# The last state's accumulation moved off VectorE, new steps, and rows of the second block split in the tail, in a Mamba and gated MLP layer on one NeuronCore

## The reference, cut

```python
x_and_res = x @ W_in.T                      # x is layernormed
xp, res = jnp.split(x_and_res, 2, axis=-1)
xc = silu(causal_conv(xp, conv_w) + conv_b) # 4 taps, each channel alone
ssm = xc @ W_x.T                            # B (16), C (16), dt (1)
dt = softplus(dt @ W_dt.T + b_dt)
h = exp(A * dt_t) * h + dt_t * B_t * xt     # for each channel and state
y_t = einsum('bed,bd->be', h, C_t) + D * xt
x = x + silu(y + res) @ W_out.T
h = silu(lin(x, w1) * s1) * (lin(x, w2) * s2)   # x is layernormed again
h = gelu(lin(h, h1) * t1)
h = gelu(lin(h, h2) * t2)
x = x + lin(h, w3) * s3
```

## Time and profile before

| | us |
|---|---|
| runs, median of 3 | 2768.11 (2767.78 to 2770.92) |
| the profiled execution | 2766.63 |
| its span, first to last instruction | 2764.8 |
| TensorE busy | 2587.6 (94%) |
| VectorE busy | 2249.4 (81%) |
| ScalarE busy | 1970.6 (71%) |
| GpSimd busy | 1770.2 (64%) |

### The profile page before, as it was taken

The page is one execution under the profiler, slowest core; times in us unless marked ns, Lnnn a source line. Parts: engine busy times, 40 slices in busy tenths (PEclk is TensorE's granted clock), DMA queues, the critical chain, the costliest instruction groups (busy, mean ns, idle before and its releaser), DMA issues.

```text
span 2764.8 us, 48560 instructions
## 1 busy us (share of the span) xinstructions
PE 2587.6 (94%) x17026; PEld 2290.3 (83%) x17026; DVE 2249.4 (81%) x2891; ACT 1970.6 (71%) x4136; POOL 1770.2 (64%) x1547
## 2 busy tenths in 40 slices
PE   6679999999999999999999999999979899999998
PEld 5558888888888888888888888888868788888887
DVE  4999999999999999999999999999982255554444
ACT  7898888888888888888888888888875222222221
POOL 3788888888888888888888888888872000000000
PEclk8899999999999999999999999999989999999999
DMA  6112112112112121121121122221231322222221
GB/s 232 43 46 71 59 60 69 58 59 66 59 62 70 62 74 62 59 70 58 59 66 59 62 67 62 73 67 59 62 115 66 122 92 80 73 92 77 92 62 32
DMA packets 130151, 198.74 MB, mean 72 GB/s; under 512 B 16368, under 2 KB 93296, under 8 KB 129904
## 3 DMA queue, kind: packets, MB, share of 16 engines
q1 hardware_dynamic: 129904, 195.57, 22.0%
HBM read 144.68 MB, written 50.86 MB: 71 GB/s over the span
## 4 chain that ended last, share of the span: by engine, by line
PE 65%; DVE 18%; issue 9%; ACT 6%; DVEq 0%; DMA 0%; POOL 0%; SPq 0%; ACTq 0%; POOLq 0%
PE banks L1434 17%; PE banks L1469 16%; PE banks L1446 10%; DVE h L1151 9%; PE banks L1346 7%; DVE acc L1164 5%; PE banks L1492 4%; PE banks L1397 4%; DVE silu L1136 3%; PE banks L1420 2%; PE banks L1357 2%; ACT banks L1022 2%; PE banks L1388 1%; PE banks L1410 0%; ACT ssm L804 0%
## 5 line engine op out<-in xcount | busy, mean ns | idle before, releaser
L1151 DVE TENSOR_TENSOR_SCAN h<-banks,ub 128x512 f32<-128x512 f32 x1024 | 1196.4, 1205 | 40.5 <-ACT banks L1022 33.7
L763 POOL TENSOR_TENSOR ub<-u,b_row 128x1020 f32<-128x1020 f32 x512 | 1214.2, 2371 | 0.3 <-issue 0.2
L1164 DVE SCALAR_TENSOR_TENSOR acc<-banks,c_tok,acc 128x512 f32<-128x512 f32 x1024 | 717.6, 735 | 76.7 <-PE banks L1446 76.6
L1022 ACT ACTIVATE banks<-dt,neg_a 128x510 f32<-128x510 f32 x1024 | 698.7, 687 | 68.7 <-DVE h L1151 67.7
L1446 PE MATMUL banks<-ident,h 128*128 128x128 f32 x4096 | 598.6, 278 | 100.3 <-DVE acc L1164 63.0
L1446 PEld LDWEIGHTS banks<-ident,h 128*128 128x128 f32 x4096 | 479.2, 142 | 189.3 <-DVE h L1151 109.2
L1434 PE MATMUL banks<-act_high,h_rounded 128*128 128x256 f32 x2048 | 512.9, 291 | 4.3 <-POOL act_low L790 3.0
L1434 PE MATMUL banks<-act_low,h_rounded 128*128 128x256 f32 x2048 | 492.9, 280 | 0.0
L1469 PE MATMUL banks<-act_high,h_rounded 128*128 128x512 f32 x1024 | 400.2, 391 | 13.2 <-DVE act_low L1213 13.2
L1469 PE MATMUL banks<-act_low,h_rounded 128*128 128x512 f32 x1024 | 400.0, 391 | 0.0
L1434 PEld LDWEIGHTS banks<-act_high,h_rounded 128*128 128x128 f32 x2048 | 387.5, 189 | 10.7 <-issue 10.0
(11 more groups left out here) (119 smaller groups left out, 4006.7 us busy)
## 6 DMA issues: line engine op xcount, KB each, us to landing
b_row<-b_scratch SPq DMA_DIRECT2D x128, 512.0 KB, 4.0
z_scratch<-z_out SPq DMA_DIRECT2D x128, 256.0 KB, 2.1
zl<-z_scratch SPq DMA_DIRECT2D x32, 1024.0 KB, 8.1
x_sb<-in_x SPq DMA_DIRECT2D x32, 256.0 KB, 4.3
x_res<-in_x SPq DMA_DIRECT2D x32, 256.0 KB, 3.4
h_full<-in_h SPq DMA_DIRECT2D x2, 4096.0 KB, 17.9
x_scratch<-x_sb SPq DMA_DIRECT2D x32, 256.0 KB, 2.9
xr<-x_scratch SPq DMA_DIRECT2D x16, 512.0 KB, 4.8
```

What stands on the lines that cost most here:

```text
L763: nc.gpsimd.tensor_tensor(ub[:, n % 2, :, 1:], u[:, :, 1:], b_row[:, n // QUARTER % 2, n % QUARTER:n % QUARTER + 1, 1:].to_broadcast([P, E ...
L1022: nc.scalar.activation(decay_half(k)[:, :, 1:], dt[:, par, 2 * i:2 * i + 2, 1:], ACT.Exp, scale=neg_a[:, n:n + 1]).then_inc(decay_ready, 1)
L1151: nc.vector.tensor_tensor_scan(h[:, n % 2, 2 * i:2 * i + 2].rearrange("p e t -> p (e t)"), banks[:, k % DECAYS, :], ub[:, n % 2, 2 * i:2 * ...
L1164: nc.vector.scalar_tensor_tensor(out=acc[:, par, q], in0=turned[q], scalar=c_tok[:, par, q, n:n + 1], in1=acc[:, par, q], op0=ALU.mult, op ...
```

## The change

The last state (n = 15) of a chunk is no longer added by VectorE. ScalarE copies each turned half times C from PSUM into `last_y`, which shares the memory of gT, at its places 2 and 3 of the next chunk. GpSimd adds `last_y` to `acc` after the products of state 2. The gate waits for that (`last_added`), and the first turned state of the new chunk waits for ScalarE's copies.

Places of all five engines are new. Block 1 of pass B is loaded in the tail, after the last chunk's gg3, and its rows go through gelu and are split in the tail; so in pass B nothing is split beside block 0. Three buffers change their addresses so that this memory is free. In the last block, the last layer takes the first half of each bank row by row as rows are split, and the result is finished and stored in two halves. The general path for weights that are not exact, which isn't run here, changes one constant.

```diff
+        acc = sb("acc", [P, 2, NT, DI], where=a_only)
...
-        acc = sb("acc", [P, 2, NT, DI], where=a_only)
         gT = sb("gT", [P, ET, T], where=a_only)
         soft = sig
+        last_y = gT[:].rearrange("p e t -> p (e t)").rearrange("p (q d) -> p q d", q=NT)
         low_bits = gT[:].rearrange("p e t -> p (e t)")
...
-        act_high[1] = sb("act_high1", [P, KH, TB], F32R, where=b_only)
...
+        act2_high = sb("act2_high", [P, KH, TB], F32R, where=b_only)
...
+        act_high[1] = sb("act_high1", [P, KH, TB], F32R, where=b_only)
...
-        act2_high = sb("act2_high", [P, KH, TB], F32R, where=b_only)
...
         PE_AT = dict(
-            norm={29: ('xn', 'xp0.a'), 31: ('xp0.b', 'xp1.a', 'xp1.b')},
-            front={0: ('conv0.a',), 1: ('conv0.b',), 2: ('conv0.c', 'conv0.d'), 3: ('conv1.a', 'conv1.b'), 4: ('conv1.c',), 5: ('conv1.d',), 10: ('ssm.a',), 11: ('ssm.b',), 13: ('dtc',), 23: ('acc0.a', 'acc0.b', 'acc0.c'), 25: ('acc1.a', 'acc1.b', 'acc1.c')},
-            post={10: ('gT0',), 13: ('gT1',), 14: ('out.a',), 16: ('out.b',), 17: ('out.c', 'out.d')},
-            mlp={32: ('yn',), 51: ('uu0.a', 'uu0.b'), 52: ('uu1.a', 'uu1.b'), 54: ('uu2.a', 'uu2.b', 'uu3.a', 'uu3.b', 'gg0.a'), 57: ('gg0.b', 'gg1.a', 'gg1.b'), 59: ('gg2.a', 'gg2.b', 'gg3.a'), 61: ('gg3.b',), 71: ('h0.a', 'h0.b', 'h0.c'), 72: ('h0.d', 'h1.a'), 73: ('h1.b', 'h1.c'), 75: ('h1.d',), 78: ('h2.a', 'h2.b'), 80: ('h2.c', 'h2.d'), 82: ('h3.a',), 83: ('h3.b', 'h3.c', 'h3.d')})
-        DVE_AT = dict(gated=(88, 88, 90, 93))
-        ACT_AT = dict(sums=4, x1=22, sums2=24, logs=6, logs2=28, xn=31, xp=(2, 5), silu=(10, 26), ssm=16, z=18, soft=21, acc=(27, 31), gT=17, high2=40, high=(66, 66, 67, 70), z_out=(77, 80, 85, 89), a_dt=31)
-        POOL_AT = dict(low2=21, x1=11, normalize=9, normalize2=17, dt=14, u=15, low=(33, 36, 34, 35))
-        SP_AT = dict(x=0, x1=12, res=12, write_b=4, b=(11, 14, 1, 6), z_out=(35, 40, 41, 44))
+            norm={27: ('xn',), 29: ('xp0.a', 'xp0.b'), 30: ('xp1.a', 'xp1.b')},
+            front={0: ('conv0.a', 'conv0.b', 'conv0.c'), 1: ('conv0.d',), 3: ('conv1.a',), 4: ('conv1.b',), 5: ('conv1.c',), 6: ('conv1.d',), 8: ('ssm.a',), 11: ('ssm.b',), 13: ('dtc',), 23: ('acc0.a',), 24: ('acc0.b', 'acc0.c'), 25: ('acc1.a',), 26: ('acc1.b', 'acc1.c')},
+            post={12: ('gT0', 'gT1'), 15: ('out.a', 'out.b'), 17: ('out.c', 'out.d')},
+            mlp={36: ('yn',), 51: ('uu0.a', 'uu0.b'), 52: ('uu1.a',), 53: ('uu1.b', 'uu2.a'), 54: ('uu2.b', 'uu3.a', 'uu3.b'), 56: ('gg0.a',), 57: ('gg0.b', 'gg1.a'), 58: ('gg1.b',), 60: ('gg2.a', 'gg2.b', 'gg3.a'), 62: ('gg3.b',), 71: ('h0.a', 'h0.b'), 72: ('h0.c', 'h0.d'), 73: ('h1.a', 'h1.b'), 74: ('h1.c',), 75: ('h1.d',), 78: ('h2.a', 'h2.b'), 80: ('h2.c', 'h2.d'), 82: ('h3.a',), 83: ('h3.b', 'h3.c', 'h3.d')})
+        DVE_AT = dict(gated=(86, 88, 92, 97))
+        ACT_AT = dict(last=(2, 3), sums=4, x1=22, sums2=24, logs=5, logs2=27, xn=31, xp=(2, 5), silu=(10, 26), ssm=16, z=18, soft=21, acc=(28, 31), gT=17, high2=39, high=(63, 66, 66, 69), z_out=(79, 80, 85, 89), a_dt=29)
+        POOL_AT = dict(last=2, low2=25, x1=11, normalize=8, normalize2=14, dt=13, u=15, low=(33, 36, 34, 35))
+        SP_AT = dict(x=0, x1=12, res=14, write_b=2, b=(8, 13, 1, 6), z_out=(39, 40, 41, 44))
 
         LAST_PIECE = {"uu": "b", "gg": "b", "h": "d", "xp": "b", "conv": "d", "ssm": "b", "acc": "c", "out": "d"}
...
+        SECOND_ROWS = ((), (0, 1, 2), (3, 4, 5), (6, 7))
...
-            ending(post, mlp, NS)
+
+            def second_rows(c, n):
+                if (c, n) == (CHUNKS + 1, NS - 1):
+                    wait_full(sp, f"gg{PAIRS - 1}", CHUNKS - 1)
+                    load_z(1)
+
+            ending(post, mlp, NS, second_rows)
...
                 wait_full(sp, f"h{PAIRS - 1}", CHUNKS - 1)
-                load_z(1)
                 load_z(2)
                 pass_a_over(sp)
...
-                    sp.wait_ge(out_e_ready, blk + 1)
-                    sp.dma_start(out_rows[:, blk], out_e[:, blk % 2]).then_inc(out_e_stored[blk % 2], 16)
+                    if blk + 1 < CB:
+                        sp.wait_ge(out_e_ready, blk + 1)
+                        sp.dma_start(out_rows[:, blk], out_e[:, blk % 2]).then_inc(out_e_stored[blk % 2], 16)
                     if blk + 2 < CB:
                         load_rows(blk + 2)
-                for slot in range(2):
-                    sp.wait_ge(out_e_stored[slot], 8 * CB)
+                for j in range(NTB // 2):
+                    sp.wait_ge(out_e_ready, CB + j)
+                    sp.dma_start(out_rows[:, CB - 1, 2 * j:2 * j + 2], out_e[:, (CB - 1) % 2, 2 * j:2 * j + 2]).then_inc(out_e_stored[(CB - 1) % 2], 16)
+                sp.wait_ge(out_e_stored[CB % 2], 8 * CB)
...
+                if n == POOL_AT["last"]:
+                    for q in range(NT):
+                        pool.wait_ge(y_added[q], NS * (c + 1))
+                    nc.gpsimd.tensor_tensor(acc[:, c % 2], acc[:, c % 2], last_y, ALU.add).then_inc(last_added, 1)
...
+                for q in range(NT):
+                    if n == ACT_AT["last"][q]:
+                        if c == 0:
+                            act.wait_ge(checked, EARLY)
+                        else:
+                            wait_full(act, "out", c - 1)
+                        act.wait_ge(turn_full[q], NS * (c + 1))
+                        nc.scalar.activation(last_y[:, q], turned[q], ACT.Copy, scale=c_tok[:, c % 2, q, NS - 1:NS]).then_inc(y_added[q], 1)
...
-                for q in range(NT):
-                    act.wait_ge(y_added[q], NS * (c + 1))
+                act.wait_ge(last_added, c + 1)
...
+                for p, rows in enumerate(SECOND_ROWS):
+                    if (c, n) == (CHUNKS + 2, ACT_AT["z_out"][p] - 2 * ACT_STEPS):
+                        for o in rows:
+                            first(1, o)
...
-                        if blk + 1 < CB:
+                        if 1 <= blk < CB - 1:
                             first(blk + 1, o)
...
-                    add_y(n)
+                    if n < NS - 1:
+                        add_y(n)
...
+                if (c, n) == (CHUNKS + 2, DVE_STEPS - 1):
+                    wait_full(dve, "out", CHUNKS - 1)
+                    for o in range(KH):
+                        split_first(1, o)
...
+                def add_rows(blk, q0, q1):
+                    dve.wait_ge(xr_in[blk % 2], 16 * (blk // 2 + 1))
+                    after(dve, out_e_stored[blk % 2], 16 * (blk // 2))
+                    nc.vector.tensor_tensor(out_e[:, blk % 2, q0:q1], prod_e[:, q0:q1], xr[:, blk % 2, q0:q1], ALU.add).then_inc(out_e_ready, 1)
...
-                    dve.wait_ge(xr_in[blk % 2], 16 * (blk // 2 + 1))
-                    after(dve, out_e_stored[blk % 2], 16 * (blk // 2))
-                    nc.vector.tensor_tensor(out_e[:, blk % 2], prod_e[:], xr[:, blk % 2], ALU.add).then_inc(out_e_ready, 1)
+                        if blk == CB - 1:
+                            add_rows(blk, 2 * j, 2 * j + 2)
+                    if blk < CB - 1:
+                        add_rows(blk, 0, NTB)
...
+                def last_rows(blk):
+
+                    into = [free(("out", blk, j)) for j in range(NTB // 2)]
+                    for i in range(2):
+                        order = [(j, k) for k in range(KH) for j in range(NTB // 2)] if i == 0 else [(j, k) for j in range(NTB // 2) for k in range(KH)]
+                        for j, k in order:
+                            if i == 0 and j == 0:
+                                pe.wait_ge(split2, KH * blk + k + 1)
+                            q = 2 * j + i
+                            for part in (act2_high, act2_low):
+                                last = nc.tensor.matmul(into[j][:, i * DIM:(i + 1) * DIM], part[:, k, q * P:(q + 1) * P], rounded["w3"][:, k],
+                                                        start=(k == 0 and part is act2_high), stop=(k == KH - 1 and part is act2_low))
+                            if i == 1 and k == KH - 1:
+                                last.then_inc(e_full, 1)
...
-                last_layer(CB - 1)
+                last_rows(CB - 1)
```

More of the change, by code:

```diff
@@ L245, in program @@
         enter_ready = sem("enter_ready")
+        last_added = sem("last_added")
         g_ready = sem("g_ready")
@@ L652, in exact @@
                         load_z(blk + 3)
-                    sp.wait_ge(out_e_ready, blk + 1)
-                    sp.dma_start(out_rows[:, blk], out_e[:, blk % 2]).then_inc(out_e_stored[blk % 2], 16)
+                    if blk + 1 < CB:
+                        sp.wait_ge(out_e_ready, blk + 1)
+                        sp.dma_start(out_rows[:, blk], out_e[:, blk % 2]).then_inc(out_e_stored[blk % 2], 16)
                     if blk + 2 < CB:
                         load_rows(blk + 2)
-                for slot in range(2):
-                    sp.wait_ge(out_e_stored[slot], 8 * CB)
+                for j in range(NTB // 2):
```

(6 more changed lines are left out.)

## The result

The changed kernel takes 2749.7 us, median of 4 runs (2747.51 to 2751.39), against 2768.27 (2767.78 to 2770.92) of the kernel before: 0.9931 times as long, with a 95% interval of 0.9913 to 0.9948. It gained 18.6 us where I had forecast 43. The profiled execution took 2750.06 us, its span 2748.1.

The account below looks back on a forecast made before the run. No engine is full; the path changes between nearly full engines within each pass A chunk. Gains of 28 - 3 + 15.4 + 2.5 = 43 us give a median of 2725 us; own range 2712 to 2738, wider range 2692 to 2754.

Parts of the forecast that it names:

- The places of the path up to the second scan of state 5: VectorE in pass A: state 0 starts at 2.1, state 3 at 13.1, state 5's second scan at 22.3 us.
- GpSimd's addition ahead of state 3: Pass A: 2.4 us addition before state 3's products, so state 3 starts half a microsecond later than before.
- GpSimd's remaining wait: Pass A: GpSimd's wait for scans falls from 7.3 to about 4 us a period.
- the 0.8 us of a gate pair: Last 10.7 us of a pass A period: one gate pair of 0.8 us is gone, leaving 9.9.
- The second block's rows: Tail: TensorE's 13.2 us wait for block 1's split rows goes, plus 2.2 us at the lower clock; 15.4 us gained.
- The last block: End of the tail: 2.0 us gap before the 64 matmuls filled, closing addition 0.5 us shorter; 2.5 us gained.
- The end of pass A: Last chunk: the new addition ahead of GpSimd's last subtractions and the later gate pair lose 3 us, between 0 and 3.5.
- the period of 62.6: Pass A: the period falls from 63.5 to 62.6 us, 0.9 a chunk, 28 us over 31 boundaries.
- ssm itself comes 0.3 to 0.4 us earlier by the pieces ahead of it on TensorE: Pass A, TensorE: ssm 0.3 to 0.4 us earlier, making the waypoint at state 13's second scan 52.7 instead of 52.8.
- VectorE's wait of 0.44 us at turned state 7: Pass A: VectorE's 0.44 us wait for the second half of turned state 7 goes.
- The last 9.8 us: Pass A, from state 13's second scan to the period's end: 9.9 us instead of 10.7.
- rival (b): Pass A gains nothing, paths through ScalarE and TensorE staying 63.5 us; the tail's 15 us alone, 2753 us; chance 0.15.

Follow-up runs that it names:

- two halves: Changed kernel with yn at 35, xp1 at 31 and GpSimd adding the last state in two halves, after the products of states 2 and 4: 2726.11 us.
- the last experiment: Changed kernel with the last block as before: all eight rows split ahead of its first matmul, one closing addition, one store: 2753.35 us.

## Why the prediction was partly wrong

**What held.** The places of the path up to the second scan of state 5 (2.1, 13.1, 22.5 for 2.1, 13.1, 22.3), GpSimd's addition ahead of state 3, GpSimd's remaining wait (2.9 us for "about 4"), and the rest of the period: from the start of ssm to the next zero it was 34.7 us before and is 34.0 after, the 0.8 us of a gate pair that I had taken off. The second block's rows gave 14.6 for 15.4. The last block gave more than 2.5: from the last matmul of the layer before to the end of the last addition it was 12.0 us before and is 9.1 after. The end of pass A lost 1.5 us for 3: from the last gate to the end of the h jobs it took 85.0 us before and 86.5 after. TensorE's wait there for GpSimd's subtractions, before and after:

```profile
PE banks L1434 <- POOL act_low L790: 3.0, 1, 3.0
```

```profile
PE banks L1472 <- POOL act_low L806: 6.5, 1, 6.5
```

With the addition nearly removed this wait was 4.4 us, and the distance 85.0 again: the addition ahead of the subtractions costs what was lost, as forecast, at half the size.

**What failed** is one term: the period of 62.6, a gain of 0.9 us over 31 boundaries, 28 us. It was 63.37, a gain of 0.14, and irregular chunks ate even that. The step is "ssm itself comes 0.3 to 0.4 us earlier by the pieces ahead of it on TensorE", with TensorE's and ScalarE's moved steps costed at nothing. I had counted the matmuls ahead of ssm and not what TensorE waits for. From the first matmul of h1 to ssm it is indeed 0.4 us less than before (11.25 for 11.68), but that matmul starts 18.15 us after zero instead of 17.12. Ahead of turned state 2 there is now less work (one convolution piece behind turned state 1 where there were two, and yn moved from place 32 to 36, behind the first half of state 2), so TensorE gets there before VectorE has done the additions and stands 1.04 us, and 0.69 at turned state 3. What was moved behind these points comes late. I had followed the scans, and not the additions that give the turned state's bank free. State 3 was half a microsecond late in my walk, but I didn't carry that on to the additions of state 2 and to turned state 3. ssm came 0.6 us later instead.

The run with the addition nearly removed shows whose 0.6 us they are: there ssm is back at 28.8, where it was before, and not earlier. So GpSimd's addition costs the 0.6, and the order of the pieces gained nothing even without it. At the end of that stretch the second scan of state 13 started 53.6 us after zero where I had 52.7; VectorE's wait of 0.44 us at turned state 7 went, as I had said, and one of 0.51 us at state 8 came in its place. The last 9.8 us were as forecast (9.9).

How this sets the period can be read from two distances in each run: from zero to the gate, and from zero to the start of ssm. In the changed kernel 43.95 us follow the gate and 33.98 the start of ssm. If each is the least that must follow, the period is the larger of the two sums. The constants are taken from the first line alone; the other lines are its test. The distances to the gate and to ssm are those of one chunk each; the medians of 23 chunks differ from them by at most 0.03 us. The last column but one is the distance from zero to the exponential behind ssm, where the two paths meet (median of 23 chunks), plus the 33.61 us that follow it in the changed kernel:

| version | zero to gate, + 43.95 | zero to ssm, + 33.98 | zero to exponential, + 33.61 | period measured |
|---|---|---|---|---|
| changed kernel | 19.42, 63.37 | 29.39, 63.37 | 29.76, 63.37 | 63.37 |
| tiny addition | 19.41, 63.36 | 28.78, 62.76 | 29.75, 63.36 | 63.38 |
| yn at 35 | 19.17, 63.12 | 29.40, 63.38 | 29.69, 63.30 | 63.35 |
| yn at 35, xp1 at 31 | 19.21, 63.16 | 29.44, 63.42 | 29.69, 63.30 | 63.34 |
| these and the tiny addition | 18.51, 62.46 | 28.52, 62.50 | 28.86, 62.47 | 62.46 |
| these and two halves | 18.51, 62.46 | 28.51, 62.49 | 29.06, 62.67 | 62.65 |
| two halves, xp1 at 30 | 18.78, 62.73 | 28.80, 62.78 | 29.12, 62.73 | 62.74 |

By the first two columns all but one come out within 0.08 us; for the two halves 0.2 is added by the wait at state 5, which delays the scans and with them the exponential (it waits 0.17 us for a scan there). By the third all seven come out within 0.05. The two paths happened to be equally long, to 0.01 us; that is chance. The outcome was my rival (b), "paths through ScalarE and TensorE stay 63.5 long", 2753 us, to which I had given 0.15. Its reason, short waits of VectorE close to the next path, was the right one. That 2749.7 us lies between 2692 and 2754 is (b)'s doing and no credit to the forecast, whose own range began at 2712 and ended at 2738.

**On the rule of the Trainium skill** (GPSIMD Engine Reference, section "Engine selection"), by which the addition belongs on VectorE: in the old places the runs agree with it (the move costs 1.4 us a chunk). In the new ones they don't: there VectorE's own addition costs 4.7 us a chunk more, since it must wait for the turned state. The lengths of the operation (2.36 us against about 1.3 for the pair) would give a loss of 1.1 us a chunk in both; that is near the first and has nothing to do with the second. On its port rule (SBUF — State Buffer, section "SBUF: two separate sides"): VectorE's additions from PSUM take 738 ns now and 735 before, with GpSimd 72 us busier, so no blocking is seen.

**Open** is what would shorten the 33.6 us behind that exponential (ScalarE's unbroken run to the second scan of state 13, 23.8 us, and 9.8 us of VectorE): no run changed that part.

## What to carry to other kernels

When several engines are nearly full, walk every queue to the next hard point, the order of the buffers' release too: a table of places that takes work from between two dependent instructions turns it into a wait, and the wait moves all that is queued behind it. Where removing a suspect entirely changes nothing, it isn't innocent yet: look for a second path of the same length and shorten both. A gap of TensorE at a change of stages is worth looking for first: here 14.6 of 18.6 us came from starting one load and its splits earlier, and most of the rest from the last block, where the last layer no longer waits for all splits.

## What the runs showed of the hardware

- The same gap of 2.0 us ahead of the last 64 matmuls cost different amounts: in the kernel before they took 7.95 us at a granted clock of 1.00, in the last experiment 9.43 us with 0.60 in the first 4 us. Without a gap it was 7.68. What makes the clock fall in one and not in the other stays open.
- The stores of 256 KB landed after 4.3 to 4.5 us in the median in all ten kernels with SyncE's new places, and after 2.1 in all four with the old ones. Two of these (the two halves, 4.4, and the same with the old places, 2.1) differ in nothing but SyncE's places. That the time goes into loads issued just ahead is my reading; no run separates it.
- The profile put the wait of 0.43 us ahead of state 1 down to ScalarE's decays. Moving xp1 on TensorE took it away, while ScalarE's exponentials stayed where they were (4.1 us after zero in both versions of the pair with xp1 at 31 and 30). The scan waits for several semaphores, the second half of turned state 15 among them (the state's buffer is written again), and that half came 1.8 us earlier. The releaser named was another engine that had ended at about the same time.
